# Graph layer pair on one core: products with W2 from float16 halves, and the last chunk of the second product in three passes by columns

## The chip, the cores and the metric

One Trainium2 chip, one NeuronCore. The metric is the device time of one launch in microseconds; the time shown for the kernel before is the median of its runs. Engines are called PE (TensorE, matmul), PEld (its weight loads), DVE (VectorE), ACT (ScalarE), POOL (GpSimd) and SP (SyncE). SPq and ACTq are rows in which these queues issue a DMA.

## The reference, cut to what matters

```
# x: (4096, 512), adj: (4096, 4096), all float32
x1  = layernorm(x + softmax(q @ k.T * scale + adj + adj) @ v)      # layer 0
h   = relu(adj @ (x1 @ W1) + b1)                                   # W1: (512, 128)
out = adj @ (h @ W2) + b2                                          # W2: (128, 512)
x   = layernorm(x1 + out)                                          # layer 1
```

The kernel reorders the last product: it forms z = adj @ h (4096 x 128) first and then z @ W2. Wide products are not done in float32. Each operand is written as a float16 "hi" half and a float16 "lo" half (what is left after hi), and three matmuls hi·hi, hi·lo and lo·hi are summed in PSUM.

## The kernel before

The program has two large stages, both written out by hand, engine by engine, with semaphores between them. The change lies in the second.

**Stage one, up to about 1565 us,** is layer 0. It also leaves adj, transposed and split in halves, in `at_dram`.

**Stage two** holds the two products with adj, called conv 0 (giving h) and conv 1 (giving z). Each has NC = 8 chunks of CW = 512 columns of the result (four row tiles of 128 nodes). A chunk runs over KB = 8 units; a unit is one megabyte of adj halves (128 partitions x 4 rows x 8 blocks x 128, float16), and gives 12 matmuls of 512 columns into one of two PSUM banks, `acc_bank[n % 2]`. The loop variable `at` counts halves of a unit, NB = 16 in a chunk. Fifteen units fit in SBUF (`slots`). SP loads them from `at_dram` (L411) and waits on `p_unit` for the slot to come free, so it runs ahead of PE by as much as the slots and the DMA allow.

After a chunk n of conv 1, ACT takes z out of the bank (`z_out`, L905, four instructions that also scale each 128-column tile by its own factor `inv_z`). PE multiplies each of the four tiles by W2 (`o_rows`, L648, one float32 matmul of 512 columns), at halves 4, 7, 10 and 13 of the next chunk (`O_AT`). For each output tile, DVE adds the residual and takes the mean and variance (`o_stats`, L1276 to L1282), POOL makes scale and shift (L1345 to L1348) and then adds b2 to the residual of the tile three further on (`residual`, L1335), ACT normalises (`o_normalise`, L887), issues the store (L894), and issues the load of the residual four tiles on (L890). There are 32 output tiles, 0 to 31; tiles 24 to 27 come of chunk 6 and are multiplied during chunk 7, and tiles 28 to 31 come of chunk 7, after which there is no more adj work to cover them.

Each engine takes its instructions in the order of the program. On ACT an instruction that waits holds all that is behind it, DMA issues too.

Of the kernel before, what the change touches and what calls it, by code (L numbers as in the profile page):

```python
# [6 lines left out]
F32 = mybir.dt.float32  # L7
F16 = mybir.dt.float16
# [7 lines left out]
P = 128  # L16
# [28 lines left out]
P_UP = 2.0 ** 12  # L45
X1_UP = 2.0 ** 10
Y_DOWN = 2.0 ** -18

CW = BANK
NC = N // CW  # L50
# [9 lines left out]
KEYS = [list(range(KB)), ORDER[0]]  # L60
TAIL = NS - KB
OUT_AT = 1
H_AT, H_OUT_AT = 4, 5
X1_LAST = 8
Y_EARLY = 3
# [47 lines left out]
    return at  # L113


def output_rows(n):
    t = TW * ORDER[1][n // TW] + n % TW
    return slice(P * t, P * (t + 1))


def gnn_program(nc, x, adj, wq, bq, wk, bk, wv, bv, w1, b1, w2, b2, out, x1_dram, g_dram, at_dram, y_dram):
    with ExitStack() as ctx:
        def sb(name, shape, dt):
            return ctx.enter_context(nc.sbuf_tensor(name, shape, dt))

        def sem(name):
            return ctx.enter_context(nc.semaphore(name))

        def flat(ap):
# [25 lines left out]
        a_sum = sb("a_sum", [P, 2, KB], F32)  # L155
        bias = sb("bias", [P, 2], F32)
        a_row = sb("a_row", [P, NT], F32)
        a_all = sb("a_all", [P, NT], F32)
        e_a = sb("e_a", [P, NT], F32)
        s_a = sb("s_a", [P, NT], F32)  # L160
# [11 lines left out]
                 "e_h", "s_h", "b1_s", "ab1", "minus_half", "minus_one"]  # L172
        sc = sb("sc", [P, len(names)], F32)
        col = {name: sc[:, i:i + 1] for i, name in enumerate(names)}

# [53 lines left out]
        z_f = [ring[:, 4 + i, :] for i in range(Z_RING)]  # L229
# [9 lines left out]
        def queries_bank(n):  # L239
# [4 lines left out]
        y_bank = bank[6]  # L244
        acc_bank = bank[0:2]
        o_bank = [bank[2], bank[3], bank[7]]
        at_bank = bank[2:4]
        ht_bank = bank[4:6]
        x1t_bank = bank[7]
# [19 lines left out]
        p_pre, p_v, p_g, p_qk, p_pv, p_y, p_adj, p_x1, p_unit, p_h, p_o = (  # L269
            sem("p_" + s) for s in "pre v g qk pv y adj x1 unit h o".split())  # L270
# [219 lines left out]
        def _(pe):  # L490
# [149 lines left out]
            def o_rows(n):  # L640
                k, i = divmod(n, TW)
                if n == 0:
                    pe.wait_ge(d_late, 32)
                if i == 0:
                    pe.wait_ge(a_z, k + 1)
                if n >= 3:
# [4 lines left out]
            for at in range(2 * HALVES):  # L651
                n, b = divmod(at, NB)
                conv, k = divmod(n, NC)
                i, half = divmod(b, 2)
# [18 lines left out]
                    pe.wait_ge(a_hs, TW * (n - 1))  # L673
                if b == 0 and n > NC + 1:
                    pe.wait_ge(a_z, n - NC - 1)
                dst = acc_bank[n % 2][:, :].rearrange("p (i c) -> p i c", i=TW)
                for j in range(2 * half, 2 * half + 2):
                    if conv == 0:
# [12 lines left out]
            for tile in outputs[-1]:  # L691
                o_rows(tile)


        @block.scalar
        def _(act):
# [200 lines left out]
                    load_residual(n + O_RING)  # L897

            def z_out(n):
                c = ORDER[1][n]  # L900
# [9 lines left out]
            for at in range(2 * HALVES):  # L910
                n, b = divmod(at, NB)
                conv, k = divmod(n, NC)
                if at == 5:
                    y_hi(NT - 1)
                if n >= 1 and b == OUT_AT:
                    if n <= NC:
                        h_out(n - 1)
                    else:
                        z_out(n - NC - 1)
                if 1 <= n <= NC and b == H_OUT_AT:  # L920
                    h_hi(n - 1)
                if conv == 1 and k == 0 and b == NB // 2:
# [11 lines left out]
            z_out(NC - 1)  # L934
            for tile in stored[-1]:
                if tile in normed[-1]:
                    o_normalise(tile)
                store_output(tile)
            for i in range(O_RING):
                act.wait_ge(d_out[i], 16 * (NT // O_RING))  # L940

# [2 lines left out]
        def _(dve):  # L944
# [324 lines left out]
            def o_stats(n):  # L1269
                i = n % O_RING  # L1270
                o = o_row[i]
                dve.wait_ge(p_o, n + 1)
                dve.wait_ge(g_res, n + 1)
                if n >= O_RING:
                    dve.wait_ge(d_out[n % O_RING], 16 * (n // O_RING))
                dve.tensor_tensor(o, o_bank[n % 3][:, :], x1_res[n % O_RING], ALU.add).then_inc(v_or, 1)  # L1276
                dve.wait_ge(v_or, n + 1)
                link(dve.bn_stats(bn[:, :], o))
                if n >= O_RING:
                    dve.wait_ge(g_orstd, n - O_RING + 1)  # L1280
                link(dve.bn_aggr(mv[:, i, :], bn[:, :]))
                dve.tensor_scalar(veps[:, i:i + 1], mv[:, i, 1:2], EPS, None, ALU.add).then_inc(v_ovar, 1)  # L1282

            def h_lo(c):
                dve.wait_ge(a_h, c + 1)
                dve.tensor_tensor(h_part[:, c, 1, :], ht_bank[c % 2][:, :], h_part[:, c, 0, :], ALU.subtract).then_inc(v_h, 1)  # L1286

            measured = output_plan(STATS_DELAY)
            for at in range(2 * HALVES):
                n, b = divmod(at, NB)  # L1290
                if at == 5:
                    y_lo(NT - 1)
                if 1 <= n <= NC and b == H_OUT_AT:
                    h_lo(n - 1)
                for tile in measured[at]:
                    o_stats(tile)
            for tile in measured[-1]:
                o_stats(tile)


        @block.gpsimd
        def _(pool):
# [30 lines left out]
            def residual(n):  # L1333
                pool.wait_ge(d_res[n % O_RING], 16 * (n // O_RING + 1))
                pool.tensor_tensor(x1_res[n % O_RING], x1_res[n % O_RING], b2_row, ALU.add).then_inc(g_res, 1)  # L1335

            pool.wait_ge(d_late, 32)
            for n in range(3):
                residual(n)
# [32 lines left out]
```

## Time and profile before

| | |
|---|---|
| median of 3 runs | 1943.66 us (1943.17 to 1945.62) |
| profiled execution, its own time | 1943.4 us |
| its span, first to last instruction | 1941.6 us (1.8 us lie around it) |
| PE busy | 98% of the span |
| DVE, ACT, POOL busy | 55%, 44%, 6% |
| mean granted TensorE clock | 0.995 |

PE's busy time is modelled: a matmul row lasts from its start until its results have landed, so rows overlap. The time from one start to the next is what a matmul costs PE.

### The profile page before, as it was taken

What the parts mean: (1) busy time and instruction counts of PE and PEld (TensorE: products, weight loads), DVE (VectorE), ACT (ScalarE), POOL (GpSimd) and SP (SyncE); (2) the same over time, 40 slices, a digit from 0 to 9 for tenths busy, and PEclk for the clock granted to TensorE, in tenths of its full rate; (3) what the DMA queues carried; (4) which work ended last, traced back from release to release, by engine and by line L of the source; (5) the groups of instructions that cost most, each with busy time, mean ns of one, the idle gap of its engine ahead of it and who ended that gap; (6) DMA issues with size and microseconds to landing.
All of it is one profiled execution on the core that took longest, in us unless ns stands there. A gap on an engine that the chain in (4) does not pass through costs nothing.

```text
span 1941.6 us, 25904 instructions
## 1 busy us (share of the span) xinstructions
PE 1905.0 (98%) x9008; PEld 877.2 (45%) x9008; DVE 1071.1 (55%) x2033; ACT 856.8 (44%) x1853; POOL 114.2 (6%) x206
## 2 busy tenths in 40 slices
PE   6899999999999999999999999999999999999997
PEld 3344444444444444444444444444444444444443
DVE  6776566666666666666666666666666620002223
ACT  3554455555555555555554555555555510101112
POOL 0000000000000000000000000000000000002334
PEclk9999999999999999999999999999999999999999
DMA  9565399999999999999999999999999999979995
GB/s 254 136 125 115 86 238 220 229 224 226 238 218 226 225 228 229 225 232 226 222 227 222 231 233 229 217 225 225 229 228 234 209 359 387 387 287 388 394 394 184
DMA packets 804804, 466.58 MB, mean 240 GB/s; under 512 B 649920, under 2 KB 657600, under 8 KB 804416
## 3 DMA queue, kind: packets, MB, share of 16 engines
q1 hardware_dynamic: 795168, 448.13, 92.1%
q10 hardware_dynamic: 9504, 16.79, 2.4%
q8 instruction: 71, 1.16, 0.3%
q14 instruction: 61, 0.50, 0.1%
HBM read 223.09 MB, written 92.01 MB: 162 GB/s over the span
## 4 chain that ended last, share of the span: by engine, by line
PE 94%; DVE 2%; DMA 2%; ACT 1%; SPq 1%; issue 1%; POOL 0%; ACTq 0%; POOLq 0%; DVEq 0%
PE bank L493 14%; PE bank L495 14%; PE bank L494 14%; PE bank L576 11%; PE bank L578 11%; PE bank L577 11%; PE bank L683 6%; PE bank L685 6%; PE bank L684 6%; PE bank L648 1%; DMA tsp<-tsp 1%; PE bank L500 1%; DMA adj_in<-in_L_gnn_Wk 0%; DVE x_sum L975 0%; SPq L422 0%
## 5 line engine op out<-in xcount | busy, mean ns | idle before, releaser
L792 ACT ACTIVATE tsp<-ring,sc 128x512 f16<-128x512 f32 x252 | 181.9, 722 | 623.1 <-DMA tsp<-tsp 622.8
L1133 DVE SCALAR_TENSOR_TENSOR ring<-bank,sc,adj_in 128x512 f32<-128x512 f32 x256 | 192.2, 751 | 381.2 <-PE bank L495 376.3
L576 PE MATMUL bank<-xv,tsp 128*128 128x512 f16 x1024 | 388.2, 379 | 6.1 <-DMA tsp<-tsp 5.6
L493 PE MATMUL bank<-xT,gT 128*128 128x512 f16 x1024 | 388.1, 379 | 0.0
L494 PE MATMUL bank<-xT,gT 128*128 128x512 f16 x1024 | 388.1, 379 | 0.0
L495 PE MATMUL bank<-xT,gT 128*128 128x512 f16 x1024 | 388.1, 379 | 0.0
L577 PE MATMUL bank<-xv,tsp 128*128 128x512 f16 x1024 | 388.1, 379 | 0.0
L578 PE MATMUL bank<-xv,tsp 128*128 128x512 f16 x1024 | 388.1, 379 | 0.0
L964 DVE SCALAR_TENSOR_TENSOR tsp<-adj_in,s_a,tsp 128x512 f16<-128x512 f32 x248 | 184.9, 746 | 64.1 <-ACT tsp L800 63.5
L964 DVE SCALAR_TENSOR_TENSOR tsp<-ring,sc,tsp 128x512 f16<-128x512 f32 x252 | 188.0, 746 | 6.4 <-ACT tsp L792 6.4
L784 ACT ACTIVATE ring<-ring,bias 128x512 f32<-128x512 f32 x256 | 180.9, 707 | 7.5 <-DVE bias L1150 7.5
L1141 DVE TENSOR_REDUCE r_max<-ring 128x1 f32<-128x512 f32 x256 | 175.6, 686 | 8.8
L800 ACT ACTIVATE tsp<-adj_in,s_a 128x512 f16<-128x512 f32 x248 | 175.1, 706 | 0.3 <-DVE s_a L961 0.3
L772 ACT ACTIVATE junk<-adj_in 128x512 fp8e4<-128x512 f32 x256 | 156.9, 613 | 0.0
L576 PEld LDWEIGHTS bank<-xv,tsp 128*128 128x128 f16 x1024 | 100.2, 98 | 124.4 <-DMA tsp<-tsp 7.0
L494 PEld LDWEIGHTS bank<-xT,gT 128*128 128x128 f16 x1024 | 100.2, 98 | 120.8
L493 PEld LDWEIGHTS bank<-xT,gT 128*128 128x128 f16 x1024 | 100.2, 98 | 120.8
L578 PEld LDWEIGHTS bank<-xv,tsp 128*128 128x128 f16 x1024 | 100.2, 98 | 120.8
L495 PEld LDWEIGHTS bank<-xT,gT 128*128 128x128 f16 x1024 | 100.2, 98 | 120.8
L577 PEld LDWEIGHTS bank<-xv,tsp 128*128 128x128 f16 x1024 | 100.2, 98 | 116.3
L1276 DVE TENSOR_TENSOR tsp<-bank,tsp 128x512 f32<-128x512 f32 x32 | 22.1, 692 | 133.3 <-PE bank L648 133.3
L1286 DVE TENSOR_TENSOR xv<-bank,xv 128x512 f16<-128x512 f32 x8 | 5.5, 692 | 156.7 <-ACT xv L881 156.7
(198 smaller groups left out, 2077.5 us busy)
## 6 DMA issues: line engine op xcount, KB each, us to landing
xv<-at_dram SPq DMA_DIRECT2D x66, 1024.0 KB, 11.1
adj_in<-in_adj SPq DMA_DIRECT2D x256, 256.0 KB, 3.3
at_dram<-tsp SPq DMA_DIRECT2D x248, 256.0 KB, 3.1
xT<-at_dram SPq DMA_DIRECT2D x21, 1024.0 KB, 14.0
adj_in<-at_dram SPq DMA_DIRECT2D x18, 1024.0 KB, 10.7
xv<-in_x SPq DMA_DIRECT2D x8, 1024.0 KB, 7.0
g_dram<-tsp SPq DMA_DIRECT2D x32, 256.0 KB, 4.0
gT<-g_dram SPq DMA_DIRECT2D x32, 256.0 KB, 3.6
```

Source lines behind the costliest of these rows:

```text
L493: pe.matmul(dst, ah, bh, start=(i == 0), stop=False)
L494: pe.matmul(dst, ah, bl, start=False, stop=False)
L495: last = pe.matmul(dst, al, bh, start=False, stop=(i == len(pairs) - 1))
L576: pe.matmul(dst, ah, vh, start=(kb == 0 and j == 0), stop=False)
L577: pe.matmul(dst, ah, vl, start=False, stop=False)
L578: last = pe.matmul(dst, al, vh, start=False, stop=(kb == KB - 1 and j == TW - 1))
L784: act.activation(p, p, ACT.Exp, bias=bias[:, r % 2:r % 2 + 1], scale=2.0, accum_out=r_sum[:, r % 2, kb:kb + 1]).then_inc(a_exp, 1)
L792: act.activation(p_split(e)[:, 0:BANK], p, ACT.Copy, scale=col[f"p_up{batch(TW * kb)}"]).then_inc(a_p, 1)
L800: act.activation(asp[a % 2][:, 0:BANK], adj_in[:, a % AR, :], ACT.Copy, scale=s_a[:, r:r + 1]).then_inc(a_ah, 1)
L964: return dve.scalar_tensor_tensor(dst, src, scale, hi, ALU.mult, ALU.subtract)
L1133: dve.scalar_tensor_tensor(t, s_bank[s % S_BANKS][:, :], col[f"k_l{batch(s // KB)}{batch(TW * (s % KB))}"], adj_in[:, s % AR, :], ALU.mult ...
L1141: dve.tensor_reduce(r_max[:, r % 2, kb:kb + 1], ring[:, s % RING, :], AX, ALU.max).then_inc(v_max, 1)
```

## The change

W2 is split once into float16 halves. ACT and DVE do that during chunk 1 of conv 0, after the largest magnitude in W2 has been found (DVE, then POOL across partitions). z leaves its bank as two halves too: ACT writes hi in one instruction of 512 columns with a constant scale, DVE writes lo (`z_lo`). A product with W2 is then three float16 matmuls of 512 columns. The factor for each row moves from ACT's four instructions to DVE's addition of the residual, which becomes a scalar_tensor_tensor with `inv_o`.

The last chunk of conv 1 is no longer one accumulation of 512 columns over 8 units. It is three, over all 8 units each: 256 columns (tiles 28 and 29), 128 columns (tile 30) and 128 columns (tile 31), in three banks (`PIECES`, `end_bank`). Each piece is taken out of its bank on its own (`z_end` on ACT, `z_end_lo` on DVE), and the products of tiles 24 to 30 are placed in the passes (`END_AT`: pass and unit, then tile). The tail of ACT and of DVE is written out in a fixed order.

```
+END = 2 * HALVES - NB
+PIECES = ((0, 2), (2, 1), (3, 1))
+PIECE_OF = [p for p, (_, count) in enumerate(PIECES) for _ in range(count)]
+END_AT = {(0, 3): 24, (0, 5): 25, (0, 7): 26, (1, 2): 27, (1, 6): 28, (2, 2): 29, (2, 6): 30}
...
-                pe.matmul(o_bank[n % 3][:, :], z_f[k % Z_RING][:, P * i:P * (i + 1)], w2_s, start=True, stop=True).then_inc(p_o, 1)
+                zh, zl = (z_hl[k % Z_RING][:, CW * part + P * i:CW * part + P * (i + 1)] for part in range(2))
+                product(o_bank[n % 3][:, :], [(zh, zl, w2_hl[:, 0:D], w2_hl[:, D:2 * D])]).then_inc(p_o, 1)
...
+            for piece, (first, count) in enumerate(PIECES):
+                dst = end_bank[piece][:, 0:P * count].rearrange("p (i c) -> p i c", i=count)
+                for i in range(KB):
+                    load = holds[1, NC - 1, i]
+                    slot = loads[load][2]
+                    if piece == 0:
+                        pe.wait_ge(d_unit[slot], 16 * (sum(1 for l in loads[:load + 1] if l[2] == slot) + (slot < Y_DRAM // TW)))
+                    for j in range(TW):
+                        wh, wl = h_hl[:, i, 0, j, :], h_hl[:, i, 1, j, :]
+                        rh, rl = (slots[slot][:, first:first + count, part * TW + j, :] for part in range(2))
+                        pe.matmul(dst, wh, rh, start=(i == 0 and j == 0), stop=False)
+                        pe.matmul(dst, wh, rl, start=False, stop=False)
+                        last = pe.matmul(dst, wl, rh, start=False, stop=(i == KB - 1 and j == TW - 1))
+                    if i == KB - 1:
+                        last.then_inc(p_end, 1)
+                    if (piece, i) in END_AT:
+                        o_rows(END_AT[piece, i])
+            o_rows(NT - 1)
...
-                for i in range(TW):
-                    last = act.activation(z_f[n % Z_RING][:, P * i:P * (i + 1)], acc_bank[n % 2][:, P * i:P * (i + 1)],
-                                          ACT.Copy, scale=inv_z[:, TW * c + i:TW * c + i + 1])
-                last.then_inc(a_z, 1)
+                act.activation(z_hl[n % Z_RING][:, 0:CW], acc_bank[n % 2][:, :], ACT.Copy, scale=Z_DOWN).then_inc(a_z, 1)
...
-                dve.tensor_tensor(o, o_bank[n % 3][:, :], x1_res[n % O_RING], ALU.add).then_inc(v_or, 1)
+                dve.scalar_tensor_tensor(o, o_bank[n % 3][:, :], inv_o[:, output_tile(n):output_tile(n) + 1], x1_res[n % O_RING],
+                                         ALU.mult, ALU.add).then_inc(v_or, 1)
```

PE at the end of the last chunk. Before, the last unit's 512-column matmuls (L683 to L685) are followed by the four products with W2 (L648):

```order
L683 MATMUL bank<-xT,xv 128x512
L684 MATMUL bank<-xT,xv 128x512
L685 MATMUL bank<-xT,xv 128x512
L648 MATMUL bank<-ring 128x512 x4
L122 UNCONDITIONAL_BRANCH
```

Now the third pass's 128-column matmuls (L726 to L728) stand there, and only the product of tile 31 (L508 to L510) is left behind them; the other three stand inside the passes:

```order
L726 MATMUL bank<-xT,xv 128x128
L727 MATMUL bank<-xT,xv 128x128
L728 MATMUL bank<-xT,xv 128x128
L508 MATMUL bank<-ring 128x512
L509 MATMUL bank<-ring 128x512
L510 MATMUL bank<-ring 128x512
L133 UNCONDITIONAL_BRANCH
```

ACT behind the last chunk, before: z is taken out (L905), then tiles 26, 27 and 28 are stored (L894), with the loads of the last two residuals (L890) and the normalising of 27 and 28 (L887):

```order
L905 ACTIVATE ring<-bank,a_row 128x128 x4
L894 DMA out<-tsp 128x512
L890 DMA tsp<-x_dram 128x512
L887 ACTIVATE tsp<-tsp,shift,rstd 128x512
L894 DMA out<-tsp 128x512
L890 DMA tsp<-x_dram 128x512
L887 ACTIVATE tsp<-tsp,shift,rstd 128x512
L894 DMA out<-tsp 128x512
```

Now (L951 is `z_end`, L928 normalises, L935 stores, L931 loads a residual) z of the second piece, then tiles 28 and 29, then z of the third piece, then tile 30:

```order
L951 ACTIVATE ring<-bank 128x128
L928 ACTIVATE tsp<-tsp,shift,rstd 128x512
L935 DMA out<-tsp 128x512
L928 ACTIVATE tsp<-tsp,shift,rstd 128x512
L935 DMA out<-tsp 128x512
L951 ACTIVATE ring<-bank 128x128
L928 ACTIVATE tsp<-tsp,shift,rstd 128x512
L935 DMA out<-tsp 128x512
```

So the taking out of a piece stands on ACT behind the normalising and storing of the two tiles before it.

DVE at the same place, now: the lo half of the second piece (L1030), the four instructions each of tiles 28 and 29, and the lo half of the third piece. Before, the instructions of the tiles followed one another with nothing between them.

```order
L1030 SCALAR_TENSOR_TENSOR ring<-bank,ring 128x128
L1342 SCALAR_TENSOR_TENSOR tsp<-bank,inv_o,tsp 128x512
L1345 BN_STATS bn<-tsp 128x6
L1348 BN_AGGR mv<-bn 128x2
L1349 TENSOR_SCALAR veps<-mv 128x1
L1342 SCALAR_TENSOR_TENSOR tsp<-bank,inv_o,tsp 128x512
L1345 BN_STATS bn<-tsp 128x6
L1348 BN_AGGR mv<-bn 128x2
L1349 TENSOR_SCALAR veps<-mv 128x1
L1030 SCALAR_TENSOR_TENSOR ring<-bank,ring 128x128
```

The addition of a tile stands behind the lo half of a piece that it does not read.

## Rows read from the trace of the kernel before

**Rows 1.** The page: granted clock and DMA share in 40 slices.

```profile
PEclk9999999999999999999999999999999999999999
DMA  9565399999999999999999999999999999979995
```

**Rows 2.** Chain that ended last, 1909 us to the end: start, length, what.

```profile
1909.92 0.86 PE bank L648 x2
...
1927.64 0.62 ACT ring L905 x2
...
1935.34 0.70 DVE tsp L1276
...
1938.24 0.81 ACT tsp L887
```

**Rows 3.** PE in order of time around one product with W2.

```profile
1885.39 0.38 PE L685 MATMUL bank<-xT,xv 128*128 128x512 f16 x1
1885.61 1.02 PE L648 MATMUL bank<-ring 128*128 128x512 f32 x2
1886.47 0.38 PE L683 MATMUL bank<-xT,xv 128*128 128x512 f16 x1
```

**Rows 4.** PE's first matmul of chunk 7, and of its last unit.

```profile
1903.29 0.38 PE L683 MATMUL bank<-xv 128*128 128x512 f16 x1
...
1924.85 0.38 PE L683 MATMUL bank<-xT,xv 128*128 128x512 f16 x1
```

**Rows 5.** ACT and DVE in order of time, chunk 1 of conv 0.

```profile
1596.85 0.69 DVE L1286 TENSOR_TENSOR xv<-bank,xv 128x512 f16<-128x512 f32 x1 [13.41 <-ACT xv L881]
1610.47 1.50 ACT L876 ACTIVATE ring<-bank,sc,c_all 128x128 f32<-128x128 f32 x4 [13.65 <-PE bank L685]
```

**Rows 6.** Groups by line and shape: busy, mean ns, idle before and its releaser.

```profile
L493 PEld LDWEIGHTS bank<-w_hl,x1T 128*128 128x128 f16 x4 | 0.4, 98 | 0.0
L1276 DVE TENSOR_TENSOR tsp<-bank,tsp 128x512 f32<-128x512 f32 x32 | 22.1, 692 | 133.3 <-PE bank L648 133.3
L1184 DVE SCALAR_TENSOR_TENSOR xr<-bank,sc,xr 128x512 f32<-128x512 f32 x1 | 0.8, 751 | 0.0
L964 DVE SCALAR_TENSOR_TENSOR xT<-bank,xT 128x128 f16<-128x128 f32 x2 | 0.6, 288 | 3.5 <-ACT xT L834 3.5
L881 ACT ACTIVATE xv<-bank 128x512 f16<-128x512 f32 x8 | 4.8, 597 | 43.2 <-PE bank L612 43.2
L834 ACT ACTIVATE xT<-bank 128x128 f16<-128x128 f32 x2 | 0.5, 272 | 4.0 <-PE bank L495 4.0
L1321 POOL PARTITION_ALL_REDUCE a_all<-a_row x32 | 23.6, 739 | 515.1 <-DVE a_row L1154 515.1
```

**Rows 7.** PE in order of time: twelve 128-column matmuls; the start.

```profile
24.64 0.95 PE L512 MATMUL bank<-tsp 128*128 128x1 f32 x8
...
1563.59 0.22 PE L493 MATMUL bank<-w_hl,x1T 128*128 128x128 f16 x1
...
1564.26 0.38 PE L576 MATMUL bank<-xv,tsp 128*128 128x512 f16 x1
```

**Rows 8.** ACT, DVE and POOL in order of time, from 1906 us.

```profile
1906.23 0.34 ACTq L894 DMA_DIRECT2D out<-tsp  x1
...
1928.04 0.44 ACTq L890 DMA_DIRECT2D tsp<-x_dram  x1
...
1930.95 1.27 POOL L1335 TENSOR_TENSOR tsp<-tsp,ring 128x512 f32<-128x512 f32 x1 [3.04 <-DMA tsp<-x_dram]
...
1931.78 0.69 DVE L1276 TENSOR_TENSOR tsp<-bank,tsp 128x512 f32<-128x512 f32 x1
...
1933.56 0.69 DVE L1276 TENSOR_TENSOR tsp<-bank,tsp 128x512 f32<-128x512 f32 x1
...
1937.02 0.15 DVE L1282 TENSOR_SCALAR veps<-mv 128x1 f32<-128x1 f32 x1
...
1939.08 0.34 ACTq L894 DMA_DIRECT2D out<-tsp  x1
```

**Rows 9.** Issue of the last unit's load; time to landing. Stretch 1740 to 1907: PE, ..., clock, DMA, GB/s.

```profile
L411 SPq DMA_DIRECT2D xT<-at_dram x1: 5505/5505/5505, 1888.5 to 1888.5; - x1
...
DMA to landing us min/median/max: 19.4/19.4/19.4
...
1740.00:1907.00 167.00, 167.00 (x730) 75.77 (x729) 42.02 (x97) 27.63 (x53) 53.15 (x98) 1.00 1.04 387
```

More of the change, by code:

```diff
@@ L267, in gnn_program @@
         d_out = [sem(f"d_out{i}") for i in range(O_RING)]
-        p_pre, p_v, p_g, p_qk, p_pv, p_y, p_adj, p_x1, p_unit, p_h, p_o = (
-            sem("p_" + s) for s in "pre v g qk pv y adj x1 unit h o".split())
+        p_pre, p_v, p_g, p_qk, p_pv, p_y, p_adj, p_x1, p_unit, p_h, p_o, p_end = (
+            sem("p_" + s) for s in "pre v g qk pv y adj x1 unit h o end".split())
+        a_w2, v_w2, v_z = sem("a_w2"), sem("v_w2"), sem("v_z")
         a_bias, a_xs, a_wv, a_m, a_w1, a_xt, a_v, a_gf, a_g, a_sum_s, a_exp, a_p, a_ah, a_x1, a_y, a_hs, a_h, a_z, a_o = (
@@ L903, in z_out, with z_end @@
                     act.wait_ge(p_o, TW * (n - Z_RING + 1))
-                for i in range(TW):
-                    last = act.activation(z_f[n % Z_RING][:, P * i:P * (i + 1)], acc_bank[n % 2][:, P * i:P * (i + 1)],
-                                          ACT.Copy, scale=inv_z[:, TW * c + i:TW * c + i + 1])
-                last.then_inc(a_z, 1)
+                act.activation(z_hl[n % Z_RING][:, 0:CW], acc_bank[n % 2][:, :], ACT.Copy, scale=Z_DOWN).then_inc(a_z, 1)
+            def z_end(piece):
+                act.wait_ge(p_end, piece + 1)
+                if piece == 0:
+                    act.wait_ge(p_o, TW * (NC - Z_RING))
+                first, count = PIECES[piece]
+                act.activation(z_hl[(NC - 1) % Z_RING][:, P * first:P * (first + count)], end_bank[piece][:, 0:P * count],
+                               ACT.Copy, scale=Z_DOWN).then_inc(a_z, 1)
             normed, stored = output_plan(NORM_DELAY), output_plan(STORE_DELAY)
-            for at in range(2 * HALVES):
+            for at in range(END):
                 n, b = divmod(at, NB)
@@ L921, in _ @@
                     h_hi(n - 1)
+                if at == W2_HI_AT:
+                    act.wait_ge(v_w2, 2)
+                    act.activation(w2_hl[:, 0:D], w2_s, ACT.Identity, scale=col["s_w2"]).then_inc(a_w2, 1)
                 if conv == 1 and k == 0 and b == NB // 2:
@@ L933, in _, with finish @@
                     store_output(tile)
[L934 to L937, printed above, removed]
+            def finish(tile):
+                o_normalise(tile)
                 store_output(tile)
+            for tile in range(NT - 2 * TW):
+                if any(tile in stored[at] for at in range(END, 2 * HALVES)):
+                    if any(tile in normed[at] for at in range(END, 2 * HALVES)):
+                        o_normalise(tile)
+                    store_output(tile)
+                if tile == NT - 2 * TW - 2:
+                    z_out(NC - 2)
+            finish(24)
+            finish(25)
+            z_end(0)
+            finish(26)
+            finish(27)
+            z_end(1)
+            finish(28)
+            finish(29)
+            z_end(2)
+            finish(30)
+            finish(31)
             for i in range(O_RING):
@@ L1286, in h_lo, with z_lo, z_end_lo @@
                 dve.tensor_tensor(h_part[:, c, 1, :], ht_bank[c % 2][:, :], h_part[:, c, 0, :], ALU.subtract).then_inc(v_h, 1)
+            def z_lo(n):
+                dve.wait_ge(a_z, n + 1)
+                minus_hi(z_hl[n % Z_RING][:, CW:2 * CW], acc_bank[n % 2][:, :], Z_DOWN, z_hl[n % Z_RING][:, 0:CW]).then_inc(v_z, 1)
+            def z_end_lo(piece):
+                first, count = PIECES[piece]
+                z = z_hl[(NC - 1) % Z_RING]
+                dve.wait_ge(a_z, NC + piece)
+                minus_hi(z[:, CW + P * first:CW + P * (first + count)], end_bank[piece][:, 0:P * count], Z_DOWN,
+                         z[:, P * first:P * (first + count)]).then_inc(v_z, 1)
             measured = output_plan(STATS_DELAY)
-            for at in range(2 * HALVES):
+            for at in range(END):
                 n, b = divmod(at, NB)
@@ L1294, in _ @@
                     h_lo(n - 1)
+                if at == W2_MAX_AT:
+                    dve.wait_ge(d_late, 32)
+                    abs_max(col["st_w2"], w2_s).then_inc(v_w2, 1)
+                if at == W2_SCALE_AT:
+                    dve.wait_ge(g_ar, 6)
+                    power(col["e_w2"], col["mx_w2"])
+                    scale_of(col["s_w2"], col["e_w2"]).then_inc(v_w2, 1)
+                    dve.wait_ge(v_w2, 2)
+                    link(dve.tensor_scalar(inv_o[:, :], inv_z[:, :], col["e_w2"], 1 / (TOP * Z_DOWN), ALU.mult, ALU.mult))
+                if at == W2_LO_AT:
+                    dve.wait_ge(a_w2, 1)
+                    minus_hi(w2_hl[:, D:2 * D], w2_s, col["s_w2"], w2_hl[:, 0:D]).then_inc(v_w2, 1)
+                if n > NC and b == Z_LO_AT:
+                    z_lo(n - NC - 1)
                 for tile in measured[at]:
                     o_stats(tile)
-            for tile in measured[-1]:
-                o_stats(tile)
+            z_lo(NC - 2)
+            o_stats(24)
+            o_stats(25)
+            z_end_lo(0)
+            o_stats(26)
+            o_stats(27)
+            z_end_lo(1)
+            o_stats(28)
+            o_stats(29)
+            z_end_lo(2)
+            o_stats(30)
+            o_stats(31)
         @block.gpsimd
```

33 lines of the change are left out of this document (24 added, 9 removed).

## The prediction

> **What bounds the kernel now.** The slices come first [rows 1]: the granted TensorE clock is full in all forty, and the DMA share is near full until shortly before the end. PE is busy 98% of the span, so I read the chain that ended last [rows 2]. Up to 1927.4 us it is PE. Then follow ACT (z out of its bank, from 1927.64), PE (products), DVE four times over (the last tile from 1935.34) and ACT's normalising at 1938.24. The last matmul with adj is issued until 1927.4 and the span ends at 1941.6: a tail of 14.2 us with little PE work. So two things count: PE's time per product with W2, while PE is the bound, and the tail.
>
> **The price of a product.** A float32 product holds PE from 1885.61 to 1886.47, 0.86 us [rows 3]. From the first matmul of chunk 7 to the first of its last unit are 21.56 us [rows 4], and 84 matmuls and 4 products lie between: (21.56 - 4 × 0.86) / 84 = 0.2157 us for a float16 matmul of 512 columns. Three cost 0.65. Each product saves 0.21. Tiles 0 to 23 are multiplied ahead of the last chunk under PE as the bound: 24 × 0.212 = 5.1 us. Chunk 7 starts at 1903.29 now, and at 1898.2 then.
>
> **Work that I cost at nothing.** W2's split sits in chunk 1 of conv 0. DVE is free from the end of h's lo half at 1597.5, and ACT waits 13.65 us for PE before 1610.47 [rows 5]. The split needs DVE 0.69, POOL 0.74, six small DVE steps of about 0.2, one more of 0.24, ACT 0.6 and DVE 0.75 [rows 6]: about 4.3 us of the 13. Without the cover it would cost those 4.3 once. z's halves: ACT about 0.65 and DVE 0.75, done 1.5 us after the chunk's end, and the first product stands 5 half units, 6.5 us, into the next chunk. Without cover that would be 1.5 us a chunk. The addition with a scale costs DVE 0.751 where the plain one costs 0.692 [rows 6]; ahead of the tail DVE waits 133 us for products in all, so this counts only in the tail.
>
> **The three passes, on PE.** The matmuls grow from 96 to 288, but the columns stay the same. What one of 128 columns costs is in the twelve of the last y product: 1563.59 to 1564.26, 0.67 us, 56 ns each, every one with its own weight load [rows 7]. A line through 56 at 128 and 216 at 512 gives 109 ns at 256. The passes take 10.5, 5.4 and 5.4 us, in all 21.2, where the chunk's matmuls take 20.7 now. With the products the passes end at 1898.2 + 10.5 + 2 × 0.65 = 1910.0, at 1910.0 + 5.4 + 3 × 0.65 = 1917.3, and at 1917.3 + 5.4 + 2 × 0.65 = 1923.9. PE never has more than one product left behind the last pass.
>
> **The three passes, on the other engines.** Here I take the tail's own periods. A tile costs DVE 1933.56 - 1931.78 = 1.78 us [rows 8], and 1.84 with the dearer addition. From the end of its last DVE step (1937.02 + 0.15) to ACT's normalising (1938.24) are 1.07 us of POOL. ACT has 0.84 for normalising until the store is issued at 1939.08, 0.38 for the store, 0.48 for a residual load (0.34 and 0.44 and the gaps) [rows 8]. POOL adds b2 to a residual in 1.27 us, between the statistics of two tiles. Taking out a piece of 128 columns costs ACT 0.27 and DVE 0.29 [rows 6], 0.64 with gaps; for 256 columns I take the middle between 0.27 and 0.60, and 0.29 and 0.75: 0.95.
>
> Tile 25 is multiplied after six units and one product, from 1898.2 + 7.9 + 0.65 = 1906.7, and is ready at 1907.5. DVE ends with it at 1909.35, POOL at 1910.4, ACT has stored and loaded by 1912.1. Only then can ACT take out the first piece, which PE left at 1910.0. DVE is through with its lo half at 1913.0, and with tiles 26 and 27 at 1916.7. Tile 26 has its statistics at 1914.8 and its shift at 1915.8; POOL then works on the residual of tile 29 to 1917.05 and only then on tile 27. ACT normalises 27 at 1918.05 and is free for the second piece at 1919.75, which PE left at 1917.3. DVE starts tile 28 at 1920.4 and ends with tile 29 at 1924.05; POOL has the residual of tile 31 in between, so ACT normalises 29 at 1925.5 and is free for the third piece at 1926.7, where PE left it at 1923.9. DVE starts tile 30 at 1927.35 and tile 31 at 1929.2. From there the end is as now: 1941.6 - 1935.34 = 6.26, and 0.06 for the addition. The span ends at 1935.5.
>
> **The sum.** 1935.5 against 1941.6: 6.1 us less. PE's shorter products ahead of the last chunk give 5.1 of it; the passes give about 1.0. The tail behind PE's adj work shrinks only from 14.2 to 11.6 us, since the pieces queue on ACT behind the tiles before them, and PE's adj work itself ends 24.0 us after its chunk's start before and 25.7 after. The profiled execution took 1943.4, 0.26 less than the median of the runs; I subtract from the median: 1937.5.
>
> **A rule against it.** The row shows 56 ns for a 128-column matmul with its weight load, but in a run of twelve; nothing here shows a run of a hundred. The Trainium skill, "TensorE: Matmul & The Clock Gate", section "Back-to-back issue gap", gives for a sustained stream of pairs of weight load and matmul about 81 ns at 128 columns. The same sentence gives 131 ns at 512, and this trace shows 216 there in thousands, so I give it no more than a rival's chance. By it the passes two and three would take 192 × 25 = 4.8 us longer on PE.
>
> **Rivals.** PE has 2.8 us to spare at the third piece (1926.7 - 1923.9), and 192 matmuls of 128 columns lie ahead of it. So up to 56 + 14 = 70 ns each nothing changes, and each ns above costs 0.19 us.
>
> (1) The long stream runs slower. Weight loads last 98 ns each [rows 6] and are issued 56 ns apart in the short run; eight records of one column with float32 weights, where only the loads can be the bound, take 0.95 us, 0.1 us apart [rows 7]. At a rate between, 75 to 90 ns, the kernel gains 5.1 down to 2.3 us: 1938.6 to 1941.4. At 81 ns, a value inside it, 1939.6.
>
> (2) The slower side: weight loads and matmuls take turns in the stream. 98 + 56 = 154 ns, 192 × (154 - 70) = 16.1 us, less 6.1: 10 us slower, 1953.7. It decides from 70 + 6.1 / 0.192 = 102 ns on. Against it are the twelve at 56, whose loads overlap the matmuls. At 95 to 102 the change is worth nothing.
>
> (3) The last unit comes late. Its load is issued at 1888.5 and lands 19.4 us later, at 1907.9; it is used now at 1924.85 [rows 4, 9]. The first pass reads it at 1898.2 + 7 × 1.31 + 2 × 0.65 = 1908.7, 0.8 us after. DMA is full from 1740 to 1907 with 387 GB/s [rows 9], so a faster PE does not bring it earlier. The store of tile 23 and the residual of tile 27 are issued at 1906.23 and just after [rows 8] and would be issued at some 1900.7, ahead of part of it: 0.5 MB, 1.3 us, so it lands at up to 1909.2 and PE waits up to 0.6 us. PE is 2.1 us early for the first piece, so this costs nothing unless the landing is beyond 1910.7. A residual load takes about 3 us in the free tail (1928.04 to 1930.95) but twice that under load; if tiles 24 and 25 wait for theirs, 1 to 2 us are lost. 1938.5 to 1939.5.
>
> (4) ACT's queue holds the pieces less than I reckon. The floor is PE: the third piece at 1923.9, the two tiles behind it and the last stretch, 1924.1 + 0.64 + 1.84 + 6.3 = 1932.9, that is 1935.0.
>
> (5) The change does not do what it says, if three float16 matmuls cost as much as the float32 one. They are the same kind as the thousands at 0.2157; I give it nothing apart.
>
> **How the numbers follow.** Forecast (1936.3 to 1938.5) 0.62; rival 1 0.16; rival 2, with the values from 95 ns on, 0.09, of which 0.05 slower; rival 3 0.07; rival 4 0.06. A change under 0.2%, 3.9 us, is about what a measurement cannot tell from none. The forecast, rivals 3 and 4, and half of rival 1 lie beyond it: 0.83 faster. The other half of rival 1 and part of rival 2: 0.12 the same. 0.05 slower. The range reaches from rival 4's side into rival 1: 1935.2 to 1940.6, leaving out the dearer part of rival 1, rival 2 and a little below.
>
> **What the profile after would show.** Chunk 7's first matmul near 1898.2, with 0.65 us for each product before it. Matmuls of 128 columns 56 ns apart, of 256 columns 109. The last pass ending near 1923.9, and ACT's instruction for the third piece near 1926.7, waiting for nothing of PE but standing right behind the store of tile 29. PE idle ahead of the product of tile 31. A wait for DMA of under 1 us at the eighth unit of the first pass. DVE starting on tile 31 near 1929.2. It is wrong if the 128-column matmuls are over 70 ns apart, if ACT waits for PE at a piece, or if chunk 7 starts later than 1899.

## The result and the profile after

| | before | after |
|---|---|---|
| median | 1943.66 us (1942.38 to 1945.62, 9 runs) | 1937.75 us (1935.19 to 1940.13, 9 runs) |
| ratio after/before, 95% interval | | 0.9968 (0.9959 to 0.9977) |
| profiled execution: time, span | 1943.4, 1941.6 us | 1940.13, 1938.2 us |
| first matmul of conv 1 to first of chunk 7 | 166.08 us | 161.02 us |
| first matmul of chunk 7 to the span's end (below: the tail) | 38.31 us | 37.5 us |

The change makes the kernel 0.3% faster, 5.9 us by the medians; 6.1 were forecast. The profiled execution of the changed kernel is the slowest of its nine: its first matmul of conv 0 comes at 1569.77 us, where the kernel before has it at 1567.29 and the other traces here have it between 1565.8 and 1570.1. No edit touches the work before that matmul. So I compare durations from a matmul onward, not the raw ends, and use an unedited second execution of the changed kernel ("control", below), which stands where the prediction assumed. The prediction calls "tail" only what follows PE's last matmul with adj; from here on the word means all from chunk 7's first matmul.

The page of the changed kernel has PE at the same share, with more matmuls (9232):

```profile
PE 1900.8 (98%) x9232; PEld 886.0 (46%) x9232; DVE 1081.1 (56%) x2050; ACT 854.0 (44%) x1832; POOL 115.2 (6%) x207
```

Two stretches tell where the time went. Columns: stretch, its length, busy time and instructions of PE, PEld, DVE, ACT, POOL, granted clock, DMA share, GB/s. First the kernel before, conv 1 to chunk 7 and chunk 7 to the end:

```profile
1737.21:1903.29 166.08, 166.08 (x726) 75.33 (x725) 42.02 (x97) 27.18 (x52) 51.16 (x95) 1.00 1.02 382
1903.29:1941.60 38.31, 28.01 (x113) 12.27 (x111) 13.65 (x32) 9.49 (x17) 16.35 (x34) 0.91 0.38 128
```

and the same two of the changed kernel:

```profile
1739.69:1900.71 161.02, 161.02 (x750) 73.27 (x749) 47.59 (x103) 24.38 (x34) 51.52 (x95) 1.00 1.02 382
1900.71:1938.20 37.49, 26.87 (x313) 22.29 (x311) 15.53 (x36) 8.86 (x13) 16.14 (x34) 0.92 0.52 181
```

PE is busy all through the first stretch in both, at full clock and 382 GB/s, and the stretch is 5.06 us shorter. In it tiles 0 to 23 are multiplied by W2: 5.06 / 24 = 0.211 us a product. The second stretch is only 0.8 us shorter, though PE is busy 1.1 us less there and ACT 0.6; DVE, which makes the lo halves, is busy 1.9 us more.

PE in order of time in the tail of the changed kernel (start, length, instruction, idle time before and its releaser):

```profile
1911.85 0.28 PE L726 MATMUL bank<-xT,xv 128*128 128x256 f16 x1 [0.52 <-DMA xT<-at_dram]
...
1916.47 0.22 PE L726 MATMUL bank<-xv 128*128 128x128 f16 x1
...
1919.10 0.22 PE L728 MATMUL bank<-xT,xv 128*128 128x128 f16 x1
1919.15 0.38 PE L508 MATMUL bank<-ring 128*128 128x512 f16 x1
...
1919.80 0.22 PE L726 MATMUL bank<-xT,xv 128*128 128x128 f16 x1
...
1927.07 0.22 PE L728 MATMUL bank<-xT,xv 128*128 128x128 f16 x1
...
1930.27 0.38 PE L508 MATMUL bank<-ring 128*128 128x512 f16 x1 [2.98 <-ACT ring L951]
```

From 1916.47 to 1919.10 are 48 matmuls of 128 columns, 47 spaces: 56 ns each. The product of one tile takes 1919.80 - 1919.15 = 0.65 us, against 0.86 in [rows 3]. The wait for DMA at the eighth unit is 0.5 us. The last matmul with adj is at 1927.07, and then PE stands idle for 3 us until the third piece has been taken out. ACT at the three pieces:

```profile
1915.17 0.38 ACT L951 ACTIVATE ring<-bank 128x256 f16<-128x256 f32 x1 [0.96 <-ACT tsp L928]
...
1921.01 0.81 ACT L928 ACTIVATE tsp<-tsp,shift,rstd 128x512 f32<-128x512 f32 x1 [1.33 <-POOL shift L1452]
1921.86 0.34 ACTq L935 DMA_DIRECT2D out<-tsp  x1
1922.24 0.45 ACTq L931 DMA_DIRECT2D tsp<-x_dram  x1
1922.73 0.28 ACT L951 ACTIVATE ring<-bank 128x128 f16<-128x128 f32 x1 [0.91 <-ACT tsp L928]
...
1928.33 0.81 ACT L928 ACTIVATE tsp<-tsp,shift,rstd 128x512 f32<-128x512 f32 x1 [1.33 <-POOL shift L1452]
1929.18 0.34 ACTq L935 DMA_DIRECT2D out<-tsp  x1
1929.57 0.28 ACT L951 ACTIVATE ring<-bank 128x128 f16<-128x128 f32 x1 [0.42 <-ACT tsp L928]
```

None of the three waits for PE. PE is through with the second piece at 1920.5 and with the third at 1927.1, and ACT takes them out at 1922.73 and 1929.57, each right behind a store (or a store and a load) of the tile before, whose normalising waited 1.33 us for POOL. DVE's rows at the second piece and at tiles 28 and 31:

```profile
1923.04 0.29 DVE L1030 SCALAR_TENSOR_TENSOR ring<-bank,ring 128x128 f16<-128x128 f32 x1 [3.41 <-ACT ring L951]
1923.25 0.74 DVE L1342 SCALAR_TENSOR_TENSOR tsp<-bank,inv_o,tsp 128x512 f32<-128x512 f32 x1
...
1931.91 0.75 DVE L1342 SCALAR_TENSOR_TENSOR tsp<-bank,inv_o,tsp 128x512 f32<-128x512 f32 x1
```

The first of these is the lo half of the second piece: DVE waited 3.41 us for ACT's hi half, and tile 28, whose product was long done, stood behind it. The waits of the tail (engine, buffer and line, releaser: us in total, times, longest) say the same:

```profile
DVE ring L1030 <- ACT ring L951: 10.0, 3, 3.6
...
PE bank L508 <- ACT ring L951: 3.0, 1, 3.0
...
ACT ring L951 <- ACT tsp L928: 2.3, 3, 1.0
```

DVE loses 10.0 us to the three taking-outs of ACT, and ACT waits for PE at none of them.

### The profile page after: what moved, and what is told of

It is laid out like the page before. It is cut to its first block, busy times and chain, and to the rows that moved or that the text cites. A ratio compares the mean times of both kernels' runs of the same rounds, so it can differ in the third digit from the quotient of the medians.

```text
span 1938.2 us, 26358 instructions
## 1 busy us (share of the span) xinstructions
PE 1900.8 (98%) x9232; PEld 886.0 (46%) x9232; DVE 1081.1 (56%) x2050; ACT 854.0 (44%) x1832; POOL 115.2 (6%) x207
## 4 chain that ended last, share of the span: by engine, by line
PE 93%; DVE 2%; DMA 2%; ACT 1%; issue 1%; SPq 1%; POOL 0%; ACTq 0%; POOLq 0%; DVEq 0%
PE bank L508 14%; PE bank L510 14%; PE bank L509 14%; PE bank L591 11%; PE bank L592 11%; PE bank L593 11%; PE bank L706 5%; PE bank L705 5%; PE bank L707 5%; DMA tsp<-tsp 1%; PE bank L515 1%; DMA adj_in<-in_L_gnn_Wk 0%; DVE x_sum L1041 0%; DVE ring L1030 0%; DVE tsp L1342 0%
## 5 line engine op out<-in xcount | busy, mean ns | idle before, releaser
L508 PE MATMUL bank<-xT,gT 128*128 128x512 f16 x1024 | 388.1, 379 | 0.0
L510 PE MATMUL bank<-xT,gT 128*128 128x512 f16 x1024 | 388.1, 379 | 0.0
L1030 DVE SCALAR_TENSOR_TENSOR tsp<-adj_in,s_a,tsp 128x512 f16<-128x512 f32 x248 | 184.9, 746 | 67.1 <-ACT tsp L841 66.2
L1030 DVE SCALAR_TENSOR_TENSOR tsp<-ring,sc,tsp 128x512 f16<-128x512 f32 x252 | 187.8, 745 | 6.7 <-ACT tsp L833 6.7
L508 PEld LDWEIGHTS bank<-xT,gT 128*128 128x128 f16 x1024 | 100.2, 98 | 120.8
L510 PEld LDWEIGHTS bank<-xT,gT 128*128 128x128 f16 x1024 | 100.2, 98 | 120.8
L928 ACT ACTIVATE tsp<-tsp,shift,rstd 128x512 f32<-128x512 f32 x32 | 26.0, 813 | 130.1 <-POOL shift L1452 130.1
```

Of the source, the lines that this page charges most:

```text
L508: pe.matmul(dst, ah, bh, start=(i == 0), stop=False)
L510: last = pe.matmul(dst, al, bh, start=False, stop=(i == len(pairs) - 1))
L1030: return dve.scalar_tensor_tensor(dst, src, scale, hi, ALU.mult, ALU.subtract)
```

## The experiments

"Theory" is the one of the prediction: the products' shorter time is gained in full ahead of chunk 7, and in the tail the order on ACT (each piece behind the tiles before it) holds the pieces, not PE. All times of a tail count from the first matmul of chunk 7 and come from one profiled execution each; the ratio is against the kernel before, timed beside it on the same chip. Three chips were used, one for control to act_order, one for dve_order, early30, two_pieces and small_first, and one for pool_order; the stretch from conv 1 to chunk 7 of the kernels with halves agrees to 0.01 us across them.

| kernel | median us | ratio (95%) | conv 1 to chunk 7 | tail |
|---|---|---|---|---|
| control | 1938.74 | 0.9973 (0.9962 to 0.9984) | 161.01 | 37.6 |
| halves_only | 1938.6 | 0.9972 (0.9961 to 0.9983) | 161.02 | 37.8 |
| passes_only | 1940.09 | 0.9984 (0.9975 to 0.9992) | 166.07 | 35.5 |
| act_order | 1934.97 | 0.9958 (0.9946 to 0.9970) | 161.02 | 35.5 |
| dve_order | 1937.32 | 0.9959 (0.9945 to 0.9972) | 161.02 | 35.7 |
| pool_order | 1936.9 | 0.9963 (0.9949 to 0.9977) | 161.02 | 36.9 |
| early30 | 1934.79 | 0.9946 (0.9934 to 0.9959) | 161.02 | 34.6 |
| two_pieces | 1934.45 | 0.9946 (0.9934 to 0.9959) | 161.01 | 34.0 |
| small_first | 1943.46 | 0.9991 (0.9983 to 1.0000) | 161.02 | 42.7 |

**control.** The changed kernel once more, no edit.

> The changed kernel again, on the chip of the three runs beside it. Expected 5 to 6.5 us under the kernel before. In its trace: 37.5 us from the first matmul of the last chunk to the end of the span (38.3 before), as in the profile after. This number leaves out what happens ahead of the last chunk, and is the one by which the runs are compared.

Chunk 7 starts at 1898.11, and the tail is 37.6 us: within 0.1 of the first profile's 37.5. So the 2.5 us by which that profile ended later came ahead of stage two (first matmul of conv 0 at 1567.17 here). The median is 4.7 us under before, less than the 5 to 6.5 expected and 1.2 less than the first 5.9, for the same kernel. Both intervals reach about 0.001, 2 us, to each side of their ratio, so the experiments that follow are read by their tails first. The tail itself was taken twice for this kernel only, and once for every other.

**halves_only.** The float16 products, but one accumulation of 512 columns in the last chunk, as before.

```
-            for at in range(END):
+            for at in range(2 * HALVES):
...
-            for piece, (first, count) in enumerate(PIECES):
...
-            o_rows(NT - 1)
+            for tile in outputs[-1]:
+                o_rows(tile)
```

> The float16 halves of z and W2 without the three passes: the last chunk is one accumulation of 512 columns again, its z is taken out whole, and the products of tiles 28 to 31 stand behind it. My theory: nearly the whole gain is in PE's shorter products, and the passes bring little because their pieces queue on ACT. Worked out from the rows of before: the last matmul with adj is issued 28 x 0.21 = 5.9 us earlier, then ACT 0.60, DVE 0.75 and the product 0.81, so DVE reaches tile 28 at 1924.0 where it stands at 1930.0 now; four tiles at 1.84 then cost 0.2 more. 5.8 us under before. Chunk 7 to the end: 37.6 us. Rival: the passes carry much of the gain; then this kernel is only some 3 us under before and chunk 7 to the end is 40 us.

The stretch before chunk 7 is 161.02, all of the 5.06 us, and the tail is 37.8, 0.5 shorter than before's. The chain that ended last in this kernel (start, length, what) shows the tail that the passes were to break up:

```profile
1924.51 0.61 ACT ring L923
...
1925.93 0.38 PE bank L508
...
1926.78 0.76 DVE tsp L1304
...
1932.30 0.76 DVE tsp L1304
```

One taking-out of z, one product, then DVE four tiles in a row, 1.84 us apart. The rival (40 us) falls. The whole change has 37.5 to 37.6: on top of the halves the three passes bring 0.2 to 0.3 us, which no ratio here can tell from nothing.

**passes_only.** The three passes with float32 products: z leaves each piece in ACT's instructions with `inv_z`, there are no lo halves of z or W2, and the residual is added without a factor.

```
-                product(o_bank[n % 3][:, :], [(zh, zl, w2_hl[:, 0:D], w2_hl[:, D:2 * D])]).then_inc(p_o, 1)
+                pe.matmul(o_bank[n % 3][:, :], z_f[k % Z_RING][:, P * i:P * (i + 1)], w2_s, start=True, stop=True).then_inc(p_o, 1)
...
-            z_end_lo(1)
...
-            z_end_lo(2)
```

> The three passes with float32 z and W2 (no halves, no scale in the addition, no splitting of W2). My theory: both parts bring something alone but do not add up. PE ahead of the last chunk stays as before, so chunk 7 starts as before; the pieces leave their banks by ACT alone, DVE's chain has no lo halves between the tiles. By the chain of rows this kernel is 3.5 to 4 us under before and takes 34.4 us from chunk 7 to the end. If the parts add up, passes alone must give what the change gives beyond 5.1, about 1 us, and 37.3 us from chunk 7 to the end.

The tail is 35.5: 2.8 us shorter than before's, though 1.1 us longer than expected. The reason of the miss is in DVE's rows, at tiles 28 and 29:

```profile
1922.55 0.69 DVE L1340 TENSOR_TENSOR tsp<-bank,tsp 128x512 f32<-128x512 f32 x1 [1.77 <-PE bank L664]
...
1926.15 0.69 DVE L1340 TENSOR_TENSOR tsp<-bank,tsp 128x512 f32<-128x512 f32 x1 [1.77 <-PE bank L664]
```

DVE waits for PE at each of them: their products stand 48 matmuls apart, and a float32 product inside that stream took 0.91 us, so here PE itself became the bound. What matters more: the passes by themselves are worth 2.8 us and the halves by themselves 0.5 in the tail, 3.3 if they added up, but the change as made has 0.7 to 0.8. Some 2.5 us are lost between the two parts. What passes_only lacks and the change has, in the tail, are the three lo halves on DVE; tile 30's addition there comes at 27.0 us into the tail and ahead of the last piece, at 29.4 in the changed kernel and behind it. ACT's order is the same in both, so that order alone does not explain the loss.

**act_order.** Only ACT's order in the tail: the pieces ahead of tiles 25, 27 and 29, not behind them.

```
             finish(24)
-            finish(25)
             z_end(0)
+            finish(25)
             finish(26)
-            finish(27)
             z_end(1)
+            finish(27)
             finish(28)
-            finish(29)
             z_end(2)
+            finish(29)
```

> The changed kernel with the three takings-out of z moved one tile forward in ACT's order (behind tiles 24, 26 and 28 instead of 25, 27 and 29); nothing else. My theory: pieces two and three wait 2 to 3 us on ACT behind the tile before them though PE has long left them. Moved forward, they start when PE is through, and the end comes 2.0 to 2.6 us earlier than in the changed kernel: 8.1 to 8.8 us under before, 35.0 us from chunk 7 to the end. Rival: DVE or POOL (the residual between the statistics of two tiles) bound the tail and not ACT's order; then the time stays that of the changed kernel within 0.5 us.

The tail is 35.5, 2.1 us shorter than control's with not one instruction less. Its waits in the tail:

```profile
ACT ring L951 <- PE bank L728: 8.1, 3, 3.0
...
DVE tsp L1342 <- PE bank L510: 9.5, 5, 4.6
...
PE bank L508 <- ACT ring L951: 0.7, 1, 0.7
```

Now ACT waits for PE at every piece (in the changed kernel it waited for its own tile), and PE's wait ahead of the last product falls from 3.0 to 0.7 us. The third piece leaves 26.8 us into the tail, 28.9 in control: the whole 2.1. That ACT's queue held the pieces is shown.

**dve_order.** Only DVE's order: tile 28 ahead of the lo half of the second piece, tile 30 ahead of that of the third.

```
-            z_end_lo(1)
             o_stats(28)
+            z_end_lo(1)
             o_stats(29)
-            z_end_lo(2)
             o_stats(30)
+            z_end_lo(2)
```

> The changed kernel with DVE's lo halves of pieces two and three moved one tile back in DVE's order (behind tiles 28 and 30 instead of 27 and 29); ACT's order as in the changed kernel. In the changed kernel DVE waits 3.4 us for ACT ahead of tile 28, whose product has long been ready. My theory: the same stall has two ends, ACT's order and DVE's order. With this one alone, tiles 28 and 30 fill DVE's wait, and the tail shrinks by 1.5 to 2 us to about 35.8 us; with ACT's alone it shrank to 35.5. Rival: the piece itself is what is late, so moving DVE's part back gains nothing or makes the third piece later: 37.6 us or more.

The tail is 35.7, 1.9 us shorter. ACT takes the pieces out 14.4, 21.9 and 27.9 us into the tail (control 14.5, 22.1 and 28.9), and only the addition of tile 31 is left behind the last. So about half of the gain is that the third piece leaves 1.1 us earlier, and the rest that one tile less stands behind it. The first half is the loss that act_order removes, seen from its other end: ACT took the third piece behind tile 29, whose statistics were late since tile 28 stood on DVE behind a lo half that waited for ACT.

**pool_order.** Only POOL: it adds b2 to the residuals of tiles 29 and 30 after tile 27, and of 31 after tile 29, so that tiles 27 and 29 get their scale and shift first.

```
-                if n + 3 < NT:
-                    residual(n + 3)
+                for m in {26: [], 27: [29, 30], 28: [], 29: [31]}.get(n, [n + 3] if n + 3 < NT else []):
+                    residual(m)
```

> The changed kernel with POOL's b2 additions for the residuals of tiles 29 and 31 moved behind the statistics of tiles 27 and 29 (they stand ahead of them in the changed kernel, 1.27 us each, and lie on the chain that ended last). Rival to ACT's order: if POOL's additions bound the tail, taking two of them off the chain gives 2.4 us, 35.2 us from chunk 7 to the end. My theory: the chain passes through them only because it has nothing better; with tiles 27 and 29 earlier, ACT still comes to the piece behind their store and residual load, and the pair of additions then delays tile 28's residual work. 0.3 to 0.8 us less, some 37.0 us from chunk 7 to the end.

The tail is 36.9, 0.7 us shorter, where the rival wanted 2.4. The third piece leaves 28.2 us into the tail, 0.7 before control's. POOL's detour is a part of the delay of the second and third piece (the normalising of the tile before them waits 1.03 us for POOL here and 1.33 in the changed kernel), but the smaller one; the order on ACT and DVE is the larger.

**early30.** act_order, and further: the product of tile 30 two units earlier in the third pass, and tile 30 ahead of the third lo half on DVE.

```
-END_AT = {(0, 3): 24, (0, 5): 25, (0, 7): 26, (1, 2): 27, (1, 6): 28, (2, 2): 29, (2, 6): 30}
+END_AT = {(0, 3): 24, (0, 5): 25, (0, 7): 26, (1, 2): 27, (1, 6): 28, (2, 1): 29, (2, 4): 30}
...
-            z_end_lo(2)
             o_stats(30)
+            z_end_lo(2)
```

> The kernel with ACT's order moved forward, and in addition the products of tiles 29 and 30 moved forward in the third pass (behind units 1 and 4 instead of 2 and 6) and DVE's lo half of the third piece behind tile 30 instead of ahead of it. My theory: in that kernel DVE waits with tile 30 for the last lo half, and both tiles 30 and 31 follow it. With tile 30 done before the third piece is, only tile 31 follows: 0.8 to 1.0 us less, 34.5 us from chunk 7 to the end, 9.5 us under before. Rival: the late unit holds PE so that nothing more is to be had: 35.5 us.

The tail is 34.6: 0.9 us under act_order, as expected, and 2.9 to 3.0 under the changed kernel. The third piece leaves 26.7 us into the tail, as in act_order (26.8), and tile 31 is added at 28.3 instead of 29.2: the gain is the tile that no longer stands behind the piece on DVE. The run changes where two products stand and DVE's order at once, and does not tell the two apart.

**two_pieces.** Two passes, 384 columns (tiles 28 to 30) and 128 (tile 31), with tiles 24 to 27 multiplied in the first and 28 to 30 in the second; ACT takes the second piece out before tile 29; DVE makes the lo halves after tiles 26 and 30.

```
-PIECES = ((0, 2), (2, 1), (3, 1))
+PIECES = ((0, 3), (3, 1))
...
+END_AT = {(0, 1): 24, (0, 3): 25, (0, 5): 26, (0, 7): 27, (1, 1): 28, (1, 3): 29, (1, 5): 30}
```

> Two passes instead of three: 384 columns (tiles 28 to 30), then 128 (tile 31); the products of tiles 24 to 27 in the first pass, of 28 to 30 in the second; ACT takes the first piece out behind tile 25 and the second behind tile 28, DVE makes the lo halves behind tiles 26 and 30. My theory: the third pass is only needed to give ACT and DVE tiles early; one narrow last pass of 5.4 us hides three tiles as well if no engine's order holds the pieces. A first pass of 15.6 us also reads the last unit at about 1913, after it has landed at 1909, so PE does not wait for DMA. 34.0 to 34.6 us from chunk 7 to the end, 9.5 to 10 us under before. Rival: with only one narrow pass DVE gets three tiles at once and becomes the bound: 36 us or more.

The tail is 34.0, the shortest, with one piece fewer. ACT, POOL and DVE in order of time:

```profile
1916.31 0.49 ACT L951 ACTIVATE ring<-bank 128x384 f16<-128x384 f32 x1 [3.57 <-PE bank L728]
...
1924.26 0.28 ACT L951 ACTIVATE ring<-bank 128x128 f16<-128x128 f32 x1 [0.43 <-PE bank L728]
1924.53 1.26 POOL L1435 TENSOR_TENSOR tsp<-tsp,ring 128x512 f32<-128x512 f32 x1 [1.55 <-DMA tsp<-x_dram]
1925.95 0.75 DVE L1341 SCALAR_TENSOR_TENSOR tsp<-bank,inv_o,tsp 128x512 f32<-128x512 f32 x1 [0.95 <-PE bank L510]
```

Both pieces are taken as soon as PE leaves them, and tile 31 is added 27.4 us into the tail, 31.2 in the changed kernel. What comes late next are the last residual loads and POOL's work on them (1.55 us of wait for DMA). So pieces, products and both orders changed together here, and the run shows what the whole gives, not each part. early30 and two_pieces have the same median within 0.4 us and the same ratio, 0.9946; of the kernels here they are the fastest. Against the changed kernel (0.9968, to 0.9959 at the lower end) the intervals just meet; the tails put them 2.9 to 3.6 us ahead.

**small_first.** Passes of 128, 128 and 256 columns: tiles 28 and 29 each by itself, 30 and 31 last.

```
-PIECES = ((0, 2), (2, 1), (3, 1))
+PIECES = ((0, 1), (1, 1), (2, 2))
...
+END_AT = {(0, 3): 24, (0, 5): 25, (0, 7): 26, (1, 2): 27, (1, 6): 28, (2, 4): 29}
...
+            o_rows(NT - 2)
             o_rows(NT - 1)
```

> The changed kernel with the pieces in the order 128, 128, 256 columns; tile 29's product at the fifth unit of the last pass, and the products of tiles 30 and 31 behind it. The first pass now wants all eight units in 5.4 us and two products, so it would read the last unit at 1898.1 + 7 x 0.67 + 2 x 0.65 = 1904.1, and the unit lands at 1909.0. My theory: PE waits some 4.5 to 5 us for DMA inside the first pass, the later passes start where they start in the changed kernel (1910.4 instead of 1911.0, since the wide pass is still to come), and the last pass ends 5.4 us later relative to its start; two tiles instead of one stand behind it. About 39.5 us from chunk 7 to the end where the changed kernel takes 37.6, some 4 us under before. Rival: DMA has slack since it serves what PE asks for next; then PE hardly waits and the time is that of the changed kernel.

The direction is right, the size is missed by 3.2 us: 42.7. A first pass of 128 columns reads the units twice as fast as one of 256, and it runs into the loads. PE in order of time, and two stretches with the columns named above:

```profile
1907.19 0.23 PE L726 MATMUL bank<-xT,xv 128*128 128x128 f16 x1 [2.56 <-DMA xT<-at_dram]
...
1907.88 0.31 PE L726 MATMUL bank<-xT,xv 128*128 128x128 f16 x1
...
1910.34 0.29 PE L726 MATMUL bank<-xT,xv 128*128 128x128 f16 x1 [1.94 <-DMA xT<-at_dram]
```

```profile
1904.50:1907.50 3.00, 0.43 (x7) 0.31 (x7) 1.78 (x4) 0.00 (x0) 1.20 (x1) 1.00 1.01 388
1907.50:1913.00 5.50, 3.56 (x27) 2.48 (x25) 0.00 (x0) 1.62 (x2) 3.46 (x9) 0.50 0.45 155
```

PE waits 2.56 us for the seventh unit and 1.94 for the eighth, 4.5 in all as expected. But after the first wait the granted clock stands at 0.50, that is 1.2 GHz, from 1907.5; matmuls of 128 columns come 106 ns apart instead of 56, until 1914.4. From the eighth unit to there lie 27 of them and one product, 4.07 us; at 56 ns and 0.65 us they would be 2.2, so I estimate the clock's part of the miss at 1.9 us. The expectation had the wait for the units and not the clock. This is what rival 3 looks like when it does decide.

## Why the prediction was right

The mechanism held: PE's shorter products ahead of chunk 7, and pieces that queue on ACT in the tail. That the median came within 0.25 us of 1937.5 is in part luck, since control's is 1.0 us higher for the same kernel. Against control, which starts chunk 7 where the prediction put it:

| step of the prediction | forecast | control |
|---|---|---|
| chunk 7 starts | 1898.2 | 1898.11 |
| passes end | 1910.0, 1917.3, 1923.9 | 1910.4, 1917.7, 1924.3 |
| ACT takes out the pieces | 1912.1, 1919.75, 1926.7 | 1912.6, 1920.2, 1927.0 |
| DVE starts tiles 28, 30, 31 | 1920.4, 1927.35, 1929.2 | 1920.7, 1927.55, 1929.4 |
| span ends | 1935.5 | 1935.7 |

By its own signs the prediction would be wrong if chunk 7 started later than 1899, and in the first profile it starts at 1900.71. That execution was late before stage two: from conv 0's first matmul to chunk 7 are 330.94 us there and 336.00 before, 5.06 less. The sign should have been put as a duration.

- **The price of a product.** 0.212 forecast, 0.211 measured over 24 products. halves_only and passes_only show it from both sides (161.02 and 166.07 us for the stretch), so this cause is shown.
- **Work costed at nothing.** W2's split costs nothing: conv 0 takes 169.92 us from its first matmul to that of conv 1, before and after. Nor do z's lo halves and the dearer addition ahead of chunk 7: PE is busy 161.02 us of 161.02, with DVE at 47.6 us against 42.0.
- **The passes on PE (rivals 1 and 2).** 56 ns at 128 columns in runs of 48 and 109 at 256, as the line through [rows 7] and the 216 ns had it. Both rivals fall. The Trainium skill, "TensorE: Matmul & The Clock Gate", section "Back-to-back issue gap", has about 81 ns for a sustained stream at 128 columns; the trace disagrees, with a weight load for each matmul.
- **The queue on ACT.** The sum's largest step in the tail, and the one that act_order was made for: reordered, the pieces wait for PE and the tail is 2.1 us shorter. It was forecast from the tail's own periods, to 0.5 us at each piece.
- **A term too small.** The first piece was forecast at 1912.1 and left at 1912.6. Tile 25's statistics were to be free of POOL at 1910.4, but POOL stood waiting for the residual of tile 27 (control: 1.51 us, at 1908.63), which is loaded while the DMA is still full. Rival 3 had such waits, for the residuals of tiles 24 and 25, at 1 to 2 us and kept apart; this one came at 0.5. It shifts all that follows by 0.2 to 0.5 us.
- **The last unit (rival 3).** In the changed kernel:

```profile
L426 SPq DMA_DIRECT2D xT<-at_dram x1: 6759/6759/6759, 1891.3 to 1891.3; - x1
...
DMA to landing us min/median/max: 20.5/20.5/20.5
```

It takes 20.5 us to land where it took 19.4 [rows 9]. The forecast had 1.3 us more at most and a wait of PE of up to 0.6; PE waited 0.5. It was hidden, as reckoned: ACT came for the first piece 2 us after PE had left it. small_first, which takes this slack away, pays for it.
- **Rival 4.** Not met by the change, but by its variants. The floor was named as 1932.9 for the span, a tail of 34.7; early30 reaches 34.6. two_pieces goes below it (34.0), since the floor held only for three passes with the products where they stood.
- **The sum.** 5.1 + 1.0 forecast, 5.06 + 0.7 to 0.8 measured. The gain of the tail came out 0.2 to 0.3 short, by the term above. But it was put down to the passes, and that is wrong: halves_only has 0.5 of it without any pass, and the passes add 0.2 to 0.3.
- **Slips of the working.** The third pass ends at 1917.3 + 5.4 + 1.3 = 1924.0, not 1923.9, and the terms of W2's split add up to 4.2, not 4.3. The granted clock was not full to the end either: from 1928 to 1942 it is 0.75 in the trace of before, where PE has only the last products. Nothing in the sum hangs on these.

What the prediction did not say is that the two parts stand in each other's way: it took the order on DVE as given and never asked what the passes would bring without the lo halves. Of the 2.5 us between 3.3 (the parts alone) and 0.8 (together) act_order wins back 2.1 and dve_order 1.9. Whether the halves' remaining 0.5 us and the passes' 2.8 add up fully once both orders are mended wasn't tried; early30, with both of them changed at the third piece, has a tail 3.7 us under that of the kernel before, which speaks for it, though it moves two products too.

## What to carry to other kernels

Splitting the last accumulation, so that its end works overlap, only pays if each piece is taken out when it is ready. Engines that take instructions in order of the program put a late instruction's wait on all that stands behind it, so in a tail written out by hand look at each instruction that waits for another engine and ask whether what stands behind it could go first: here three swaps on ACT were worth 2.1 us, and the three passes without them 0.2 to 0.3. Test the parts of a change apart, since a sum of parts that exceeds the whole (3.3 against 0.8 us) points at an order to mend. And before a stage is made to read its inputs faster, compare its new first use with the landing of the last load, not with the bandwidth.

## What the hardware showed that I had not expected

- In small_first one wait of PE of 2.56 us was followed by a granted clock of 0.50 over the next rows, with 106 ns between 128-column matmuls. The tail was 3.2 us longer than expected; 1.9 of it is the clock by the estimate above, and the rest was not separated. In the changed kernel PE waits 0.5 us for the eighth unit, and the matmuls behind it keep their 109 and 56 ns.
- A load of one unit took 1.1 us longer to land when PE ran 5 us ahead of its former time (20.5 against 19.4), though both were issued under the same load of 382 GB/s. I put it down to the store and the residual load that ACT issues ahead of part of it; no run takes them away, so this stays argued. It goes with PE's pace and not with the passes: the last unit takes 20.5 us in halves_only too, and 19.2 in passes_only.
- The time before stage two differs by up to 4.2 us between executions (first matmul of conv 0 at 1565.84 to 1570.06 in the traces here), almost as much as the whole change is worth. Where it comes from was not looked into.
